# Pool scratch writes of 128x64 floats behind every gather and scatter of an expert loop

## The reference, cut to what matters

```
logits = -dist2 + jnp.einsum('bld,ed->ble', x, rw) + rb
topv, topi = jax.lax.top_k(logits, TOP_K)          # TOP_K = 4 of E = 16
w = jax.nn.softmax(topv, axis=-1)
hidden = jax.nn.gelu(jnp.einsum('bld,efd->blef', x, w1) + b1, approximate=False)   # F = 512
exp_out = jnp.einsum('blef,edf->bled', hidden, w2) + b2
sel = jnp.take_along_axis(exp_out, topi[..., None], axis=2)
fused = jnp.sum(w[..., None] * sel, axis=2)
x = x + _layernorm(fused)
```

## Time and profile before

| what | value |
|---|---|
| median of 3 runs | 615.46 us (615.41 to 619.34) |
| span of the profiled execution | 666.4 us |
| mean granted TensorE clock in it | 0.941 |
| PE busy | 525.1 us (79%) |
| DVE busy | 364.4 us (55%) |
| ACT busy | 351.7 us (53%) |
| Pool busy | 278.4 us (42%) |
| expert loop, first gather to last scatter | 229.1 to 636.7 us |

### The profile page before, as it was taken

The page is one execution under the profiler, slowest core; times in us unless marked ns, Lnnn a source line. Parts: engine busy times, 40 slices in busy tenths (PEclk is TensorE's granted clock), DMA queues, the critical chain, the costliest instruction groups (busy, mean ns, idle before and its releaser), DMA issues.

```text
span 666.4 us, 19936 instructions
## 1 busy us (share of the span) xinstructions
PE 525.1 (79%) x6242; PEld 467.0 (70%) x6242; DVE 364.4 (55%) x1325; ACT 351.7 (53%) x1079; POOL 278.4 (42%) x308
## 2 busy tenths in 40 slices
PE   4999889997241588998888987888978888788984
PEld 4957779996030267897778876877877777777832
DVE  6564769997999734655656741112245443333126
ACT  5624156774864364556557864445545455445513
POOL 4000000000262265656666665666656566665410
PEclk9999969999575599999999999899999999999988
DMA  7980000003200355555555755555777755565463
GB/s 227 244 313 21 3 2 1 0 0 127 126 2 0 125 146 162 153 151 150 156 148 145 234 146 148 143 158 146 210 223 227 215 150 147 156 190 163 146 221 111
DMA packets 55746, 92.28 MB, mean 138 GB/s; under 512 B 10352, under 2 KB 26096, under 8 KB 55152
## 3 DMA queue, kind: packets, MB, share of 16 engines
q1 hardware_dynamic: 45424, 72.35, 36.2%
q0 software_dynamic: 10240, 18.89, 9.7%
HBM read 78.07 MB, written 17.37 MB: 143 GB/s over the span
## 4 chain that ended last, share of the span: by engine, by line
PE 57%; DVE 20%; issue 10%; ACT 6%; DVEq 3%; DMA 2%; another core or an unknown queue 1%; POOL 0%; SPq 0%; POOLq 0%; ACTq 0%
PE bank L2154 22%; PE bank L2147 18%; DVE shared L1193 2%; DVE shared L1185 2%; PE bank L2139 2%; DVEq L1669 2%; DVE early L1473 2%; ACT value L889 2%; PE bank L1741 2%; DVE early L1669 2%; DMA shared<-yd 2%; PE bank L1846 1%; PE bank L1778 1%; PE bank L2095 1%; PE bank L1768 1%
## 5 line engine op out<-in xcount | busy, mean ns | idle before, releaser
L889 ACT ACTIVATE value<-bank,shared 128x128 f32<-128x128 f32 x632 | 180.3, 380 | 181.2 <-PE bank L2147 165.6
L2154 PE MATMUL bank<-shared,value 128*128 x1264 | 177.1, 283 | 53.5 <-issue 25.5
L2154 PEld LDWEIGHTS bank<-shared,value 128*128 128x128 f32 x1264 | 154.1, 192 | 72.9 <-issue 72.2
L2147 PE MATMUL bank<-early,shared 128*128 x1264 | 173.0, 280 | 3.1 <-ACT early L897 1.9
L597 POOL DMA_INDIRECT shared<-xd,early x128 | 124.8, 975 | 87.7 <-PE bank L2147 45.5
L606 POOL DMA_INDIRECT yd<-early x128 | 126.2, 986 | 82.9 <-PE bank L2147 41.5
L2147 PEld LDWEIGHTS bank<-early,shared 128*128 128x128 f32 x1264 | 154.4, 192 | 7.0 <-issue 6.1
L1669 DVE SCALAR_TENSOR_TENSOR early<-bank,value,early 128x128 f32 x158 | 55.4, 351 | 188.9 <-PE bank L2154 115.5
L560 POOL TENSOR_TENSOR shared<-shared,xn 128x512 f32<-128x512 f32 x4 | 5.1, 1266 | 174.4 <-DVE xn L1268 166.6
L2009 PE MATMUL bank<-ksp,shared 128*128 128x32 bf16 x1536 | 41.1, 177 | 0.0
L2009 PEld LDWEIGHTS bank<-ksp,shared 128*128 128x128 bf16 x1536 | 40.2, 97 | 0.1
(11 more groups left out here) (334 smaller groups left out, 684.6 us busy)
## 6 DMA issues: line engine op xcount, KB each, us to landing
shared<-w1b SPq DMA_DIRECT2D x158, 258.0 KB
w1b<-in_w_t SPq DMA_DIRECT2D x1, 4096.0 KB, 17.4
shared<-col_dram SPq DMA_DIRECT2D x1, 4096.0 KB, 13.0
shared<-in_w_t SPq DMA_DIRECT2D x1, 4096.0 KB, 12.4
att<-yd SPq DMA_DIRECT2D x8, 512.0 KB
shared<-yd SPq DMA_DIRECT2D x4, 1024.0 KB, 9.0
xd<-xnT SPq DMA_DIRECT2D x2, 1280.0 KB
shared<-xd,early POOLq DMA_INDIRECT x128
```

The lines of the kernel that those rows point to most:

```text
L889: ins = act.activation(hT[:, i % 2, tok(c)], bank[2 + i % 2][:, tok(c)], ACT.Gelu, bias=w1_now[:, i % WR, F + c:F + c + 1])
L2147: ins = mm(bank[2 + i % 2][:, tok(c)], w1_now[:, i % WR, tok(c)], x_now, start=True, stop=True)
L2154: ins = mm(bank[6 + i % 2][:, 0:D], hT[:, i % 2, tok(c)], w2_sb[:, bass.ds(e, 1), c, :] .rearrange("p a d -> p (a d)"), start=(c == 0), st ...
```

## The change

A scratch area `spare` of four places, each 128 partitions by 64 floats, is taken out of `value` ahead of `hT` (so `hT` and `own` lie 256 floats further on). Behind each gather and each scatter Pool writes zeros to one of the four places, in turn. The write raises `const_step`; it waits, from the fifth one on, only for the write four before it, which used the same place. Nothing reads `spare`.

```
--- before.py
+++ after.py
@@ -251,6 +251,7 @@
             return valf[:, work[0] - width:work[0]]
 
         xg = shared[:, WR * WB:WR * WB + XR * XW].rearrange("p (a d) -> p a d", a=XR)
+        spare = of_work(2 * D).rearrange("p (a d) -> p a d", a=4)
         hT = of_work(2 * F).rearrange("p (a f) -> p a f", a=2)
         own_f = of_work(SLOTS * 2 * E)
         own = own_f.rearrange("p (a n) -> p a n", a=SLOTS)
@@ -583,6 +584,13 @@
 
 
             moved = [0]
+            first = steps[0]
+
+            def space():
+                n = steps[0] - first
+                freed(pool, const_step, steps[0] + 1 - 4 if n >= 4 else 0)
+                steps[0] += 1
+                pool.memset(spare[:, n % 4, :], 0.0).then_inc(const_step, 1)
 
             def in_step():
                 freed(pool, up_ps, (moved[0] - HEAD) * IALL // (2 * JALL))
@@ -597,6 +605,7 @@
                 pool.indirect_dma_start(out=xg[:, n % XR, :], out_offset=None, in_=xd[n // JT][:, :],
                                         in_offset=bass.IndirectOffsetOnAxis(ap=idx_src[:, n:n + 1], axis=0))\
                     .then_inc(xg_in[n % XSEM], 16)
+                space()
 
             def results(m):
                 in_step()
```

## The result

The changed kernel takes 618.40 us (median of 20 runs, 613.37 to 621.68) against 614.28 us for the kernel before, timed beside it (median of 20, 610.75 to 619.34). The ratio is **1.0065, 95% interval 1.0040 to 1.0091**: 4.0 us slower, between 2.5 and 5.6. That is less than the 1% that the prediction called telling, but it is not nothing.

A forecast was written before the change was run, and what follows sets the result against it. TensorE (PE) was taken to pace Pool, hiding the writes' 256 x 0.15 = 38 us under 84 us of Pool waits; 615.5 us plus 0.5 at the loop's start gave 616.0 us, range 612 to 648.

The forecast's parts named there:

- What one scratch write costs: On Pool, per memset behind an indirect DMA: 0.09 to 0.15 us taken, outer bounds 0 and 0.45 us.
- The lower outer bound: Per write on Pool: 0 us, if the write falls inside the idle 0.30 us of issue between two indirect DMAs.
- The slack to watch: Pool in the loop: 1.60 us per DMA at PE's pace less 1.27 unwaited leaves 0.33 us.
- The unexplained 50.9 us: Profiled execution over the median, place unknown; if all in the loop and on PE, PE allows 1.40 us per DMA.
- The wait that is added: On Pool, a write's wait for the one four before: three DMAs, at least 3.8 us, lie between; it never holds.
- Where it is hidden: Pool's added 38 us under 84 us of waits: loop start costs 0.3 to 0.9 us, middle swallowed, end 0.
- The lead of 5 us: Mid loop: lateness Pool's DMAs must use up before others wait; scatter 95's slots were given about 6 us.
- The squeezed pace: Rival: unprofiled loop leaves Pool 1.40 to 1.48 us per DMA, a write costs 0.15 to 0.20; 616 to 629, chance 0.13.
- Own issue gap: Rival: between DMAs the write needs another 0.30 us gap, pace 1.72 us; 641, 672 or 692 us, chance 0.18.
- Cold start: Rival: a DMA behind ordinary Pool work takes 1.73 us against 0.95, pace 2.20, about 770 us; chance 0.05.
- VectorE in the way: Rival: DVE and Pool stall each other, 0.12 us more per write, pace 1.54; counted in the squeezed pace.
- What would show it: Profile signs: memsets 0.1 to 0.2 us, spacing 1.36 to 1.42, L2147 waits 87 to 50, stretch 408, PE's DMA waits about 1.

The follow-up runs named there:

- second profile: The kernel before, no edit, timed and profiled again: ratio 1.0022, span 614.3 us, first to last indirect DMA 349.3 us.

## Why the prediction was right, and where it was not

The range (612 to 648) holds the 618.4 us, and no telling difference, within about 1%, was the likeliest case. The size was not right: 0.5 us were forecast and 4.0 measured, and that the total came so near is in part luck, since two errors worked against each other. Point by point:

- **What one scratch write costs.** 0.09 to 0.15 was taken, 0.033 is what the spacing shows. The lower outer bound, a write inside the gap of issue, was nearer. The argument for leaving it (ordinary Pool instructions show no gap) was about the wrong pair. The gap stands ahead of a DMA, and in the rows the write lies in its front part. What remains, 0.16 us, stands between the write's end and the DMA. The rule of the Trainium skill (Perfetto Trace Analysis, GPSIMD Engine Instruction), to time by spacings, holds here too: the write's row reads 0.168 us and its spacing cost 0.033. I had applied it to the memset alone, not to the pair.
- **The slack to watch.** This is the step that failed: "0.33 us per DMA", from 1.60 - 1.27. The 1.60 came from an execution with a held-up loop. The second profile gives 1.370 - 1.277 = 0.09 us on average, and 1.287 - 1.277 = 0.01 from DMA 114 on. The unexplained 50.9 us were named, and the case in which all of it lay in the loop, with 1.40 us per DMA, was near the true one; but the cause was not the profiler.
- **The two errors cancelled** in part. With 0.15 us and no slack over 134 DMAs the forecast would have been 20 us, as the waited write shows (0.144 us more spacing than the kernel before, and 1.0336, some 20 us, in time).
- **The wait that is added.** Right that it never holds. Four DMAs lie between a write and the one four before it, not three, which gives it more room still.
- **Where it is hidden.** Start: DMA 6 still waits for PE (1.39 us idle in place of 1.65), as said, and the run with the first 110 writes costs nothing. Middle: "the next wait swallows it" holds up to DMA 113 and fails behind it, where there is no next wait. The lead of 5 us at the slots of scatter 95 did not exist in the undisturbed loop, before the change or after it, as VectorE's waits for a landing show. End: right, nothing is lost behind the last y_add.
- **The rivals.** The squeezed pace is what happened, with a smaller write and a smaller slack than I priced. Its range of 616 to 629 holds the result. Own issue gap: wrong; the write starts at the DMA's end and 0.17 us stand behind it, and even the write four times as wide keeps the spacing at 1.471, far from 1.72. Cold start: wrong; gathers and scatters behind a write have medians of 0.98 and 0.99 us, against 0.97 and 0.98 in the earlier trace rows, and 1.73 is the first DMA of every trace. A few later ones take up to 1.70 us, but so they do without the writes (1.69 in the second profile). VectorE in the way: the writes have 0.168 us on average and 0.25 at most, so nothing of the 0.12 per write that I allowed for.
- **What would show it.** The memset rows are as said (0.17 us); the spacing (1.310, not 1.36 to 1.42), the stretch (352.9 us, not 408) and PE's waits for DMA (3.5 us, not about 1) are not. I named the waits for L2147 as the sign. They fall from 30.4 us (11.4 + 19.0, second profile) to 19.6 us. The sign for the rival, "no waits for PE any more", was too strict: what counted was whether waits remain behind a given point, not how many there are in all.

What held up the first profiled execution stays open. From the eighth y_add to the last it takes 2.49 us per step against 2.12 in the second profile, longer in both halves of the loop, at nearly the same mean clock (0.941 and 0.938); down waits there for ScalarE and for nothing shown.

## What to carry to other kernels

In this kernel the engine that issues work for the others had slack only up to the last place where it waited; behind that every 0.03 us counted. So read such an engine's waits along time and not as a sum. A profile whose span is 8% above the median of the plain runs describes another execution than the one that is timed: ask for a second one, or treat its spacings as an upper bound, before a slack is taken from it. A short instruction that nothing waits for lay here in the gap ahead of an indirect DMA for 0.03 us; the same with a wait behind it cost four times as much (0.144).

## What the runs showed of the hardware

- Between two indirect DMAs of Pool that don't wait are 0.30 us. A memset put there lies in part inside them: with 1, 64 and 256 columns of 128 partitions the unwaited spacing is 1.279, 1.310 and 1.471 us, against 1.277 without. From 64 to 256 columns that is 0.161 / 192 = 0.00084 us per column, as in the earlier trace rows; from 1 to 64 only 0.0005, as if part of it were still hidden.
- A wait of Pool for its own write's semaphore adds 0.11 us to the spacing (1.310 to 1.421).
- The same kernel, at a mean granted clock of 0.94 in both, had one profiled execution of 666.4 us and one of 614.3 us. What differed is not known.
